# Sixty-four experts on one NeuronCore: copies between partition groups shared 12 to 4 between ScalarE and VectorE in the second half, and the row-list parts moved

## The reference

```python
top_val, top_idx = lax.top_k(probs, TOP_K)                 # 8 of 64 experts for each of 4096 rows
...
gu = lax.ragged_dot(xs, jnp.swapaxes(gate_up_proj, 1, 2), group_sizes)      # (rows, 1024) x (1024, 768)
gate, up = jnp.split(gu, 2, axis=-1)
hact = jax.nn.silu(gate) * up                                               # (rows, 384)
y = lax.ragged_dot(hact, jnp.swapaxes(down_proj, 1, 2), group_sizes)        # (rows, 384) x (384, 1024)
out = jnp.zeros_like(x).at[tok].add(y * w[:, None])
```

## Time and profile before

| | us |
|---|---|
| median of 3 runs | 7631.97 |
| lowest and highest | 7624.85, 7641.91 |
| the profiled execution | 7641.59 |
| its span, first to last instruction | 7640.0 |
| PE busy | 6934.0 (91%) |
| DVE busy | 5077.5 (66%) |
| ACT busy | 4237.5 (55%) |
| POOL busy | 1856.8 (24%) |

### The profile page before, as it was taken

How to read it: one execution, slowest core, us unless ns; L and a number is a source line. 1 busy time by engine, 2 the same in 40 slices (tenths; PEclk the granted TensorE clock), 3 DMA queues, 4 the chain that set the end, 5 groups by cost and what they waited for, 6 DMA issues and landing times.

```text
span 7640.0 us, 118234 instructions
## 1 busy us (share of the span) xinstructions
PE 6934.0 (91%) x35662; PEld 5665.2 (74%) x35664; DVE 5077.5 (66%) x9136; ACT 4237.5 (55%) x8202; POOL 1856.8 (24%) x1602
## 2 busy tenths in 40 slices
PE   7998998998995999992999999999999999999998
PEld 5777777777774887771777777777777777777777
DVE  5666666666664344437777777777777777777777
ACT  4666666666664122211665656666656665666665
POOL 1122122122110000000333333333333333333333
PEclk9999999999997999995999999999999999999999
DMA  2222222222212221221565555555555555556555
GB/s 73 54 66 59 54 66 58 55 66 57 55 50 81 91 67 66 76 75 42 147 182 157 158 154 166 172 156 165 160 156 165 160 158 160 161 161 166 160 158 151
DMA packets 313830, 875.34 MB, mean 115 GB/s; under 512 B 44128, under 2 KB 85600, under 8 KB 313568
## 3 DMA queue, kind: packets, MB, share of 16 engines
q1 hardware_dynamic: 214640, 506.45, 20.8%
q0 software_dynamic: 98928, 365.58, 20.2%
HBM read 614.84 MB, written 206.70 MB: 108 GB/s over the span
## 4 chain that ended last, share of the span: by engine, by line
PE 36%; DVE 9%; issue 4%; DMA 2%; ACT 1%; DVEq 0%; POOL 0%; ACTq 0%; POOLq 0%
PE ps_gu L1941 10%; PE ps_gu L1943 10%; PE ps_gu L1942 10%; DVE pieces L2270 3%; DVE xs_lo L2280 2%; DVE logits L2222 2%; PE ps_xe L1961 1%; PE ps_y L1941 1%; PE ps_y L1942 1%; PE ps_y L1943 1%; DMA xt_rows<-rows,gather_t 1%; DVE x_rows L2274 1%; PE ps_l L1950 1%; ACT xs_hi L2083 1%; DVE act_s L2332 1%
## 5 line engine op out<-in xcount | busy, mean ns | idle before, releaser
L1941 PE MATMUL ps_gu<-xs_hi,gu_hi 128*128 128x512 f32 x3072 | 1236.9, 403 | 97.6 <-DVE gu_lo L2322 97.5
L1943 PE MATMUL ps_gu<-xs_hi,gu_lo 128*128 128x512 f32 x3072 | 1227.5, 400 | 0.0
L1942 PE MATMUL ps_gu<-xs_lo,gu_hi 128*128 128x512 f32 x3072 | 1223.3, 398 | 0.0
L2075 ACT ACTIVATE pieces<-x_rows 32x256 f32<-32x256 f32 x2080 | 872.9, 420 | 216.8 <-DVE x_rows L2274 150.9
L2270 DVE COPY pieces<-x_rows 32x256 f32<-32x256 f32 x2080 | 767.8, 369 | 31.9
L1941 PEld LDWEIGHTS ps_gu<-xs_hi,gu_hi 128*128 128x128 f32 x3072 | 589.6, 192 | 238.9 <-DVE gu_lo L2322 115.0
L1920 POOL TENSOR_TENSOR dn_lo<-raw_w,dn_hi 128x512 fp32r<-128x512 f32 x384 | 491.1, 1313 | 1009.7 <-ACT dn_hi L2122 1009.7
L1942 PEld LDWEIGHTS ps_gu<-xs_lo,gu_hi 128*128 128x128 f32 x3072 | 589.8, 192 | 128.2
L1943 PEld LDWEIGHTS ps_gu<-xs_hi,gu_lo 128*128 128x128 f32 x3072 | 589.5, 192 | 127.9
L890 DVE TENSOR_TENSOR pt_lo<-ps_t,pt_hi 128x512 fp32r<-128x512 f32 (+3 forms) x768 | 425.3, 554 | 377.9 <-ACT pt_hi L711 373.7
L455 PE MATMUL ps_qkv<-xt_hi,w_hi 128*128 128x512 f32 x1512 | 620.3, 410 | 18.1 <-ACT proj L611 10.4
(11 more groups left out here) (333 smaller groups left out, 16468.0 us busy)
## 6 DMA issues: line engine op xcount, KB each, us to landing
raw_w<-w_gu SPq DMA_DIRECT2D x384, 512.0 KB
raw_w<-w_down SPq DMA_DIRECT2D x192, 512.0 KB
w_raw<-wqkv SPq DMA_DIRECT2D x192, 256.0 KB, 2.6
turned<-proj SPq DMA_DIRECT2D x512, 64.0 KB, 2.0
out<-residual SPq DMA_DIRECT2D x36, 512.0 KB, 2.6
q_hi<-q_hi SPq DMA_DIRECT2D x128, 128.0 KB, 2.3
attn_out<-out_t POOLq DMA_DIRECT2D x128, 128.0 KB, 2.3
residual<-x SPq DMA_DIRECT2D x32, 512.0 KB, 4.7
```

Of the source, the lines that this page charges most:

```text
L1941: pe.matmul(out, a_hi, w_hi, start=first, stop=False)
L1942: pe.matmul(out, a_hi, w_lo, start=False, stop=False)
L1943: return pe.matmul(out, a_lo, w_hi, start=False, stop=last)
L2075: mv = act.activation(pieces[32 * q:32 * q + 32, i % 2, a, :].rearrange("p (k c) -> p k c", c=32), quarter(a, i, q), ACT.Copy)
```

## The change

In supers 0 and 1, ACT and DVE keep 8 copies each. In supers 2 and 3 ACT makes 12 (a = 0, 1, 2) and DVE 4 (a = 3). `move_half` is now `move_rows`, `half_moved` is `act_moved`, and `moved` is `dve_moved`. ACT does all of super 2's copies and none of super 3's ahead of `split_h(2)`; 9 of super 3's stand behind the first two `split_super`s and the last 3 behind `finish(0)`. On DVE list part 1 moves from ahead of `multiply(2)` to ahead of `multiply(1)`; parts 2 and 3 move up to either side of turn 3.

```diff
+        def moved_by_act(i):
+
+            return (0, 2) if i < 2 else (0, 1, 2)
+
+        def moved_by_dve(i):
+
+            return (1, 3) if i < 2 else (3,)
...
                 for q in parts:
-                    for a in range(0, Q4, 2):
+                    for a in moved_by_act(i):
                         mv = act.activation(pieces[32 * q:32 * q + 32, i % 2, a, :].rearrange("p (k c) -> p k c", c=32), quarter(a, i, q), ACT.Copy)
...
                 silu_of(2)
-                move_half(e + 1, 2)
-                move_half(e + 1, 3, range(2))
+                move_rows(e + 1, 2)
                 split_h(2)
                 split_super(e + 1, 0)
                 split_super(e + 1, 1)
-                move_half(e + 1, 3, range(2, Q4))
+                move_rows(e + 1, 3, range(3))
                 finish(0)
+                move_rows(e + 1, 3, range(3, Q4))
                 split_super(e + 1, 2)
...
             def turn_super(n, i):
                 dve.wait_ge(rows_s[i], (n + 1) * 16)
                 for q in range(Q4):
-                    for a in range(1, Q4, 2):
+                    for a in moved_by_dve(i):
...
                 turn_super(e + 1, 0)
+                list_part(after, 1)
                 multiply(1)
...
-                list_part(after, 1)
                 multiply(2)
                 rest_of_h(2)
                 rest_of_super(e + 1, 0)
                 keep_weights(e + 1)
                 turn_super(e + 1, 2)
                 rest_of_super(e + 1, 1)
+                list_part(after, 2)
                 turn_super(e + 1, 3)
+                list_part(after, 3)
                 rest_of_super(e + 1, 2)
-                list_part(after, 2)
                 rest_of_super(e + 1, 3)
-                list_part(after, 3)
                 end_list(after)
```

More of the change, by code:

```diff
@@ L1793, in experts @@
         yl_ps, yl_ok, wl_ok, sl_ok = (m.sem(n) for n in ("yl_ps", "yl_ok", "wl_ok", "sl_ok"))
-        half_moved = m.sem("half_moved")
-        moved = m.sem("moved")
+        act_moved = m.sem("act_moved")
+        dve_moved = m.sem("dve_moved")
         rows_s = [m.dma_sem(f"rows_s{i}") for i in range(SUP)]
@@ L2067, in _, with move_rows @@
         def _(act):
-            def move_half(n, i, parts=range(Q4)):
+            def move_rows(n, i, parts=range(Q4)):
                 act.wait_ge(rows_s[i], (n + 1) * 16)
@@ L2073, in move_half @@
                 for q in parts:
-                    for a in range(0, Q4, 2):
+                    for a in moved_by_act(i):
                         mv = act.activation(pieces[32 * q:32 * q + 32, i % 2, a, :].rearrange("p (k c) -> p k c", c=32), quarter(a, i, q), ACT.Copy)
                 if parts[-1] == Q4 - 1:
-                    mv.then_inc(half_moved, 1)
+                    mv.then_inc(act_moved, 1)
             def split_super(n, i):
@@ L2102, in _ @@
             act.activation(warm[:, :], warm[:, :], ACT.Silu)
-            move_half(0, 0)
+            move_rows(0, 0)
             for i in range(SUP):
                 if i + 1 < SUP:
-                    move_half(0, i + 1)
+                    move_rows(0, i + 1)
                 split_super(0, i)
@@ L2154, in super_block @@
                 split(5)
-                move_half(e + 1, 0)
+                move_rows(e + 1, 0)
                 silu_of(1)
-                move_half(e + 1, 1)
+                move_rows(e + 1, 1)
                 split_h(1)
@@ L2268, in turn_super @@
                 for q in range(Q4):
-                    for a in range(1, Q4, 2):
+                    for a in moved_by_dve(i):
                         mv = dve.tensor_copy(pieces[32 * q:32 * q + 32, i % 2, a, :].rearrange("p (k c) -> p k c", c=32), quarter(a, i, q))
-                mv.then_inc(moved, 1)
-                dve.wait_ge(moved, START + n * SUP + i + 1)
-                dve.wait_ge(half_moved, START + n * SUP + i + 1)
+                mv.then_inc(dve_moved, 1)
+                dve.wait_ge(dve_moved, START + n * SUP + i + 1)
+                dve.wait_ge(act_moved, START + n * SUP + i + 1)
                 dve.transpose(x_rows[:, i, 0:H].rearrange("p (k i b) -> p i k b", i=Q4, b=32),
```

## The result

The changed kernel takes 7666.2 us (median of 6 runs, 7652.3 to 7672.7) against 7634.7 (6 runs, 7624.9 to 7641.9): a ratio of 1.0039, 95% interval 1.0027 to 1.0052. It is slower by 0.4%, about 30 us, where a gain of 51 was forecast. The two profiled executions differ by less, 7659.8 against 7640.0 us of span: the one of before is at the top of its runs, the one of after near the bottom of its own. 5.3 us of those 19.8 are there before any changed instruction runs. In all thirteen traces of this document that unchanged part ends between 3563 and 3579 us, latest in after, so a difference of spans of this size is not the change's alone.

The account below looks back on a forecast made before the run. DVE looked like the bound; after the change, scatter 0's landing and ACT's path to the next start. -24 (33 starts), -31 (30 tail experts) and +4 (tail wait, end) made -51 us: 7581 us, range 7547 to 7614.

Parts of the forecast that it names:

- Term 1: DVE, list part 1 leaving the place ahead of multiply(2): multiply(2) 1.13 us earlier, PE's hs_lo wait from 1.36 to about 0.23.
- Term 2: DVE, turns 2 and 3: 8 copies fewer take 2.4 us off its chain from hs_lo to gu_lo.
- Term 3: ACT, 8 copies more at 0.43 us: 9 instead of 4 ahead of finish(0), which begins 1.02 us later.
- the rival of the slow copies: ACT's copies slow to 0.62 us each, putting finish(0) later: +116 us, so slower at 7748 us; chance 0.05.
- Term 4: PE's third group, overwriting the tile finish(0) reads: slack of 1.1 us used up, a wait of about 0.1.
- Term 5: Next start through ACT, 33 experts without tail: 0.72 us gained each, -24 us; number of half-clock starts unchanged.
- Term 6: The 30 experts with a tail: -31 us inside, +3 for PE's wait on gathered rows, +1 at the end.

Follow-up runs that it names:

- third_buffer: The changed kernel with finish(2) writing into a third buffer, so that it waits for no scatter: 7454.4 us, ratio 0.9764 to the kernel before.
- finish0_first: The changed kernel with one line moved, finish(0) ahead of all of ACT's copies of super 3: 7447.2 us, ratio 0.9751 to the kernel before.
- no_scatter_1: The changed kernel without the scatter of group 1 and the waits for it: 7632.9 us, ratio 0.9996 to the kernel before.
- lists_only: The kernel before with the list parts alone moved, copies 8 and 8 as before: 7639.9 us, ratio 1.0007 to the kernel before.
- no_scatter_2: The changed kernel without the scatter of group 2; finish(2) still waits for scatter 0: 7601.0 us, ratio 0.9954 to the kernel before.
- buffer_before: The kernel before with a third buffer for finish(2), so that it waits for no landing: 7621.8 us, ratio 0.9981 to the kernel before.
- copies_only: The changed kernel with the list parts back in their old places, copies 12 and 4: 7749.0 us, ratio 1.0153 to the kernel before.
- first_splits: The changed kernel with ACT's first two weight splits of the next expert ahead of its two register loads: 7579.5 us, ratio 0.9930 to the kernel before.
- finish0_old_list: finish0_first with the list parts back in their old places: 7540.8 us, ratio 0.9878 to the kernel before.

## Why the prediction was wrong

The moves inside an expert and the bound were forecast rightly. None of the three signs of being wrong that the prediction named was seen (gu_lo waits gone, hs_lo still at 1.3, a wait on y_sup):

- Term 1: multiply(2) comes 12.58 after multiply(1), 13.71 before: 1.13 as forecast, and the wait fell to 0.22 (0.23 forecast).
- Term 2: DVE is no longer last; ACT's gu_hi ends its idle time ahead of gu_lo.
- Term 3: finish(0) 0.89 later (1.02 forecast). ACT's copies kept their speed, so the rival of the slow copies was not what happened, although its sign did.
- Term 4: no wait on the tile at all (0.1 forecast).
- The landing sets finish(2) in every expert: it begins 0.10 us after the landing in all 64, before and after. third_buffer and finish0_first show it.

Three steps failed, all where a quantity was carried over or put at nothing.

**Term 5, "to gu_hi 2.42".** It carried the distance from finish(2) to gu_hi over from the kernel before; it is 3.11 after. The 0.7 more is ACT's register load, 1.12 instead of 0.41. In the kernel before that load begins 2.4 us (mean) after POOL has ended the instruction of scatter 1, in after 1.6. Scatter 1 goes out 1.15 later now: finish(0) is 0.89 later, and between it and finish(1) three copies (1.29) stand where ACT had waited 1.08 for DVE. POOL's instruction for it also takes 2.14 us instead of 1.6. A load that begins 1.5 to 2.5 us behind that end is done 2.64 to 2.84 us behind it (seven kernels), whenever it began, down to its usual 0.28: so of beginning 0.8 sooner 0.7 is paid back. no_scatter_1 shows that the scatter is the cause. So the 33 experts gained 0.19 each at the start, not 0.72: -6 us, not -24.

**Term 5, "I change its count by nothing".** PE is done 1.1 earlier and starts 0.2 earlier, so its pause went from 2.7 to 3.6 us in the mean, not to 3.0. The half clock then came at 30 starts (27 before), and in 13 cases instead of 2 it lasted 6.8 us. What each costs can be read from the time from such a start to multiply(1), which is 23.41 us where the clock stays up (6 starts before, 3 after), 25.0 with 3.4 us of half clock (25 before, 17 after) and 25.8 to 26.2 with 6.8 us (2 before, 13 after). In the mean that time grew by 0.41 over the 33 starts behind a pause and by 0.02 over the 30 behind a tail: 14 us, and 1.5 in the first expert. The forecast counted starts at half clock and held the length of each to be fixed. That part is read from the two traces; no run changed the clock alone.

**Term 6, "It goes out about 0.8 earlier while PE comes 1.0 earlier".** The gather did go out earlier (1.1 us). But what PE waits for is the landing, and it follows scatter 2's: 2.5 us behind it in after, 2.3 before (some of that scatter's completions are missing in the trace of before; lists_only, with the kernel's old order on ACT, has 2.4). no_scatter_2 shows it from the other side. Scatter 2 is 0.8 us later through finish(2), so the rows are 0.5 later (39.04 after multiply(1) in place of 38.51) and the tails' wait took all of the 1.1 that PE had won, and a little more: from multiply(1) on, 30 x 0.14 = +4 us where -28 was forecast. The order was known, for the prediction itself puts the gather behind the third scatter on POOL; but it reckoned the gather's issue only and gave its landing no term.

The sum again, for the profiled execution: -6 (starts), +16 (clock), +4 (tails), +1 (end) = +15, with the 5 us ahead of the changed code the 19.8 between the two spans. Against the forecast, -51, the starts are 18 off, the clock 16 and the tails 32. The medians are 32 apart, 12 more than the spans; no trace here accounts for these. Of the three only the number of starts at half clock stood in the bounds (10 us either way): those varied the terms that were written down, and each miss was a quantity taken as fixed. A net gain of 0.7% that rests on a second path, whose timing before was only half seen since it was not the last, did not carry a chance of 0.86.

The figure that the prediction weighed (the Trainium skill, DMA: Bandwidth & Descriptors, "Anatomy of one DMA — SWDGE (gpsimd) path"), an estimate of 3.2 us to landing for 512 KB, did not hold here: scatter 0 lands 6.3 us after its issue in before and in after.

## What to carry to other kernels

When a profile shows that a landing sets the next step, ask first what stands ahead of the instruction that starts the transfer: moving finish(0) ahead of nine copies was worth 219 us, while the change as it stood, with the copies shared out better between the two engines, cost 32. When work is taken from the last engine to another, check what the second engine's extra work delays on its way to a DMA issue, and reckon transfers by their landing behind the ones queued ahead, not by their issue. When PE finishes earlier and its next start stays where it is, the pause between them grows, and the half clock behind it can last longer: that is a term of its own.

## What the runs showed that was not expected

- A register load from `starts` by ACT takes 0.28 us as a rule. Begun 1.0 to 1.5 us after POOL has ended the instruction of a 512 KB scatter it takes 1.13 to 1.36; begun 1.5 to 2.5 us after, it ends 2.64 to 2.84 us after, so it takes 1.17 down to 0.3; later than that it is 0.28 again (all kernels but no_scatter_1). Begun while that instruction is still running it takes 0.28, but 0.63 in third_buffer, where it begins 0.05 us after the instruction. In buffer_before it is 1.15 in the 33 experts and costs nothing, since DVE is last there. Without scatter 1 it is never above 0.48.
- The tail's gather, queued behind scatter 2, lands 2.3 to 2.7 us after that scatter, whether issued 1.9 or 3.8 us behind it (before, after, copies_only, first_splits, finish0_first). Without the scatter it lands 4.40 after its own issue. The distance is not fixed: in buffer_before the gather is issued 4.2 us behind the scatter and lands 2.0 behind it, 4.43 after its own issue, so nearly as if alone; in finish0_old_list it is issued 3.2 behind and lands 1.9 behind.
- The time of scatter 0 to its landing is 6.3 us in the mean with or without scatter 1 behind it.
- After a longer pause the half clock lasted longer (115 us in 29 stretches against 170 in 34). In after's 13 long cases it set in 1.2 to 1.7 us ahead of the start, so during the pause, and lasted 6.8 us; in the 17 others it set in between 0.4 ahead of the start and 1.5 behind it and lasted 3.4.
- How many of the 33 starts show the half clock goes with the mean pause ahead of them: none at 1.4 us (finish0_old_list), 4 at 1.7 (first_splits), 25 to 27 at 2.7 (before, lists_only, buffer_before), 21 at 2.8 (no_scatter_1), 30 to 32 at 3.6 to 3.7 (after, copies_only, no_scatter_2).
